# A decoder layer: the product of the context's value and output weights in three rounded products instead of full f32

## Time and profile before

| what | value |
| --- | --- |
| median of the runs shown | 452.72 us |
| the profiled execution's own time | 452.99 us |
| its span in the profile | 451.2 us |
| PE busy | 437.0 us, 97% |
| DVE, ACT, POOL busy | 304.8, 300.9, 210.9 us |

### The profile page before, as it was taken

How to read it: one execution, slowest core, us unless ns; L and a number is a source line. 1 busy time by engine, 2 the same in 40 slices (tenths; PEclk the granted TensorE clock), 3 DMA queues, 4 the chain that set the end, 5 groups by cost and what they waited for, 6 DMA issues and landing times.

```text
span 451.2 us, 11055 instructions
## 1 busy us (share of the span) xinstructions
PE 437.0 (97%) x3657; PEld 394.4 (87%) x3657; DVE 304.8 (68%) x1243; ACT 300.9 (67%) x927; POOL 210.9 (47%) x246
## 2 busy tenths in 40 slices
PE   8999999999999999999999999999999999999991
PEld 7888898989989898898988989899889999999970
DVE  3376666787797575868678677969797734333495
ACT  3688666576777668566686665868665686776535
POOL 1899499250103112210237635375733587666521
PEclk9999999999999999999999999999999999999997
DMA  5960121400210001020001214122023654343675
GB/s 147 323 197 3 64 94 46 142 1 1 95 47 1 1 2 36 24 62 23 1 25 59 83 48 118 48 66 76 26 72 96 165 176 141 121 128 118 215 268 196
DMA packets 26543, 40.16 MB, mean 89 GB/s; under 512 B 3199, under 2 KB 17683, under 8 KB 26483
## 3 DMA queue, kind: packets, MB, share of 16 engines
q1 hardware_dynamic: 21532, 27.86, 20.2%
q0 software_dynamic: 3408, 9.33, 5.8%
q10 hardware_dynamic: 1547, 2.27, 1.7%
HBM read 26.83 MB, written 12.61 MB: 87 GB/s over the span
## 4 chain that ended last, share of the span: by engine, by line
PE 86%; DVE 6%; DMA 3%; ACT 1%; issue 1%; POOL 1%; SPq 1%; ACTq 0%; POOLq 0%
PE bank L310 18%; PE bank L311 18%; PE bank L312 18%; PE bank L829 8%; PE bank L879 7%; PE bank L840 7%; DMA ex_raw<-y_dram 2%; PE bank L1033 2%; PE bank L1057 2%; PE bank L780 2%; PE bank L935 1%; PE bank L757 1%; PE bank L1043 1%; PE bank L1065 1%; DVE stats L1581 1%
## 5 line engine op out<-in xcount | busy, mean ns | idle before, releaser
L1219 ACT ACTIVATE probs<-probs,negmax 128x128 f32<-128x128 f32 x256 | 99.7, 393 | 24.6 <-DVE negmax L1493 24.6
L1493 DVE CUSTOM_DVE_ANT_0 probs<-bank,mask 128x128 f32<-128x128 f32 x256 | 62.4, 285 | 45.5 <-PE bank L829 45.5
L310 PE MATMUL bank<-w_hi,ot_hi 128*128 (+1 forms) x284 | 80.6, 284 | 0.1
L311 PE MATMUL bank<-w_lo,ot_hi 128*128 (+1 forms) x284 | 80.3, 283 | 0.0
L312 PE MATMUL bank<-w_hi,ot_lo 128*128 (+1 forms) x284 | 80.1, 282 | 0.0
L1504 DVE TENSOR_TENSOR probs<-probs,rsum 128x512 f32<-128x512 f32 x64 | 58.7, 917 | 2.2
L310 PE MATMUL bank<-xt_hi,w_hi 128*128 128x512 f32 (+1 forms) x148 | 59.7, 403 | 0.0
L611 POOL DMA_INDIRECT xg_dram<-xacc,place x32 | 33.6, 1051 | 54.4 <-PE bank L840 29.6
L311 PE MATMUL bank<-xt_lo,w_hi 128*128 128x512 f32 (+1 forms) x148 | 57.6, 389 | 0.0
L312 PE MATMUL bank<-xt_hi,w_lo 128*128 128x512 f32 (+1 forms) x148 | 57.5, 389 | 0.0
L310 PEld LDWEIGHTS bank<-w_hi,ot_hi 128*128 128x128 f32 x284 | 54.0, 190 | 0.5 <-issue 0.5
(11 more groups left out here) (252 smaller groups left out, 1056.4 us busy)
## 6 DMA issues: line engine op xcount, KB each, us to landing
qkv<-xg_dram SPq DMA_DIRECT2D x39, 128.5 KB, 2.2
ex_raw<-in_w_experts SPq DMA_DIRECT2D x18, 256.0 KB
w_raw<-in_w_quads SPq DMA_DIRECT2D x10, 256.0 KB, 4.7
xacc<-in_x SPq DMA_DIRECT2D x4, 512.0 KB, 4.1
ex_raw<-in_w_cross SPq DMA_DIRECT2D x4, 512.0 KB, 3.9
w_raw<-in_ctx_t_in ACTq DMA_DIRECT2D x4, 512.0 KB, 3.8
w_raw<-in_w_quads SPq DMA_DIRECT2D x3, 512.0 KB, 6.1
xacc<-in_x_t SPq DMA_DIRECT2D x3, 512.0 KB, 6.9
```

The lines of the kernel that those rows point to most:

```text
L310: pe.matmul(o, a_hi, b_hi, start=first, stop=False)
L311: pe.matmul(o, a_hi, b_lo, start=False, stop=False)
L1219: nc.scalar.activation(tile, tile, ACT.Exp, scale=-1.0, bias=negmax[:, s.par, h, j:j + 1], accum_out=sums[:, s.par, h, j:j + 1]).then_inc( ...
L1493: nc.vector.tensor_tensor_reduce(probs[:, s.par, h, slices(j, P)], sc_bank[h][:, slices(j, P)], mask[:, :], -SCALE, 3.0e38, ALU.add, ALU.m ...
```

## The change

The three products hi hi, hi lo and lo hi of `three` take the place of one full f32 product, four times in each of four steps. POOL splits each block of ex_raw into w_hi and w_lo, in the place of the shared expert (block `NE` = 8, which no quad uses, and which split_expert(0) and (1) fill later). PE waits for the split (cross_split) instead of the load, load_cross waits for the split instead of the product, and POOL's split waits for PE's step before, since it overwrites w_hi. The steps move from behind slots 3 to 6 to behind slots 5 to 8, take_wvo from behind slot 7 to behind slot 8, and wvo_low from inside slot 8 to inside slot 9. The ten row casts of split_rows become join_rows, with split_cross(1) ahead of them.

```diff
@@ load_cross
                 if b > 0:
-                    sp.wait_ge(wvo_step, b)
+                    sp.wait_ge(cross_split, b)
                 sp.dma_start(ex_raw[:, :, :], w_cross[b]).then_inc(in_cross, 16)
@@ gpsimd
+            def split_cross(r):
+                pool.wait_ge(in_cross, 16 * (r + 1))
+                if r > 0:
+                    pool.wait_ge(wvo_step, r)
+                split(w_hi[:, NE, :, :], w_lo[:, NE, :, :], ex_raw[:, :, :], cross_split)
+
@@ split_rows
                     pool.wait_ge(pool_step, 6 + 2 * k)
+            def join_rows():
+                pool.wait_ge(cross_split, 2)
+                raw = rows_raw.rearrange("p (e n) -> p e n", n=D)
                 for r in (32, 96):
                     for k in range((NX + 1) // 2):
@@ gpsimd, the order
             split_part(3, 2)
+            split_cross(0)
             nc.gpsimd.memset(rows_raw, 0.0).then_inc(rows_zeroed, 1)
             tables()
             split_rows()
+            split_cross(1)
+            join_rows()
             add_ob(1)
+            split_cross(2)
             add_ob(2)
+            split_cross(3)
             split_ctx(0)
@@ cross_weights
-                pe.wait_ge(in_cross, 16 * (r + 1))
+                pe.wait_ge(cross_split, r + 1)
                 for i in range(2):
                     for m in range(KT):
-                        mm = pe.matmul(bank[7][:, slices(m, D)], ex_raw[:, 0, i * D + m * P:i * D + (m + 1) * P],
-                                       ex_raw[:, 1, slices(i, D)], start=(r == 0 and i == 0 and m == 0),
-                                       stop=(r == G - 1 and i == 1), skip_group_check=True)
+                        here = slice(i * D + m * P, i * D + (m + 1) * P)
+                        v_hi, v_lo = w_hi[:, NE, 0, here], w_lo[:, NE, 0, here]
+                        o_hi, o_lo = w_hi[:, NE, 1, slices(i, D)], w_lo[:, NE, 1, slices(i, D)]
+                        begin, end = r == 0 and i == 0 and m == 0, r == G - 1 and i == 1
+                        for n, (v, o) in enumerate(((v_hi, o_hi), (v_hi, o_lo), (v_lo, o_hi))):
+                            mm = pe.matmul(bank[7][:, slices(m, D)], v, o, start=(begin and n == 0),
+                                           stop=(end and n == 2), skip_group_check=True)
                 mm.then_inc(wvo_step, 1)
@@ tensor
-            behind = {3 + r: [lambda r=r: cross_weights(r)] for r in range(G)}
+            behind = {5 + r: [lambda r=r: cross_weights(r)] for r in range(G)}
@@ scalar
-            behind = {1: [make_sel], 7: [take_wvo, lambda: load_ctx(0)]}
+            behind = {1: [make_sel], 7: [lambda: load_ctx(0)], 8: [take_wvo]}
@@ vector
-            inside, small = {SPG: [wvo_low]}, {}
+            inside, small = {SPG + 1: [wvo_low]}, {}
```

More of the change, by code:

```diff
@@ L245, in decoder_program @@
         in_xt0 = [sem(f"in_xt0_k{k}") for k in range(KT)]
-        in_quad = [sem(f"in_quad_{n}") for n in "qkvo"]
+        in_quad = [sem(f"in_quad_{n}") for n in "qkv"]
         q_split, k_split, v_split = sem("q_split"), sem("k_split"), sem("v_split")
@@ L272, in decoder_program @@
         bias_moved = sem("bias_moved")
+        cross_split = sem("cross_split")
         rows_zeroed, in_up_rows, in_rows, rows_ready = (sem("rows_zeroed"), sem("in_up_rows"), sem("in_rows"),
```

## The result

Over 20 runs each, the changed kernel took 454.01 us in the median (452.92 to 456.29), the kernel before 453.07 (451.92 to 454.55). The ratio is 1.0026, with a 95% interval of 1.0014 to 1.0039: slower by 1.2 us by the ratio (0.9 by the medians), where 1.0 was forecast. How it comes about is as forecast in the main: PE's steps are shorter, and PE waits for POOL's splits at the third or the fourth of them. How the stalls divide between those two differs from one execution to the next, and one cost was not foreseen at all.

A forecast was written before the change was run, and what follows sets the result against it. PE, busy 97% of the span, was taken to bound the kernel until 322 us. Stalls of 2.3 us less a gain of 1.28 put 1.0 on 452.72, giving 453.7 us, range 451.3 to 455.7.

The forecast's parts named there:

- PE's own gain: PE's four cross_weights steps: 1.82 us becomes 1.50 each, a gain of 0.32 a step, 1.28 us in four.
- When PE asks: Behind slots 5 to 8: PE, without stalls, asks for the four splits at 63.6, 73.7, 84.0 and 94.1 us.
- POOL's chain: GpSimd's queue of splits, row casts and sums: splits ready at 45.45, 73.4, 85.6 and 96.4 us.
- the third pair: split_cross(2) on POOL, a cast and a subtraction: 3.7 us with the gap, ready at 85.6.
- the upper bound: POOL's late case: pairs at 4.0, rows at 52.6, 1 us of collisions; fourth split about 98.9, +3.5 us.
- The stalls: PE waits for POOL's splits: 1.6 us at the third step, another 0.7 at the fourth, 2.3 in all.
- the margin at the second split: split_cross(1) ready at 73.4 against PE's asking at 73.7: no stall, 0.3 us of margin.
- the upper end of POOL's chain: Fourth split at about 98.9 us with pairs, rows and collisions at their slow ends: +3.5 us.
- rival 2: Slot 9: DVE becomes 1.5 us late at add_cross(0,0), PE waits 0.9 more, 454.6 us; chance 0.1.
- PE's cover: DVE's products beside POOL's subtractions may last up to 2.4 + 0.7 us; costed at nothing while PE has no wait.
- Costed at nothing: take_wvo, wvo_low in DVE's slot 9, load_ctx(0), split_ctx(0) and load_expert(0): later, but covered, so no cost.
- a gain of half a microsecond for the rows: SP's queue: load_cross(1) goes at 45.5, so the row loads go from 47.8, 0.5 us earlier.

The follow-up runs named there:

- the version without stalls: Changed kernel, GpSimd takes split_cross(2) between the halves of the row casts and split_cross(3) ahead of add_ob(2): 451.39 us, ratio 0.9963; again 451.45 us, 0.9967.
- that with the third step's alone: Changed kernel with split_cross(3) ahead of add_ob(2) on GpSimd: 453.50 us, ratio 1.0012.

## Why the prediction was right

- *PE's own gain*, 0.32 a step: 0.29 measured in the trace (1.53 for 1.82), and by the runs 1.6 us in four steps, against 1.28.
- *When PE asks*: 63.6, 73.7, 84.0 forecast, 63.8, 73.9, 84.2 measured. The 0.2 is where PE stood at slot 3's end.
- *POOL's chain*: right in its order and links, and light by 1.2 us at the third split. Two terms were mis-sized: the ten row casts, 7.0 for 6.3, and the third pair, 1.53 + 2.88 = 4.5 with the gap for 3.7, both beside DVE's products. They are partly made up for by a second split 0.4 us earlier than forecast. I took the means and gave the collisions to the upper bound alone.
- *The stalls*: "PE stalls 1.6 us" at the third step was 2.7 in one execution and 0.3 in the other; "another 0.7 us" at the fourth was 0 in the one and 0.68 in the other. They trade against each other: all in all 2.7 us in the one, and in the other 1.3, the 50.94 us from slot 4 to slot 9 less the 49.61 of the version without stalls. By the ratios, the version without any stall is at 0.9963 and 0.9967, that with the third step's alone at 1.0012, the changed kernel at 1.0026 and 1.0029: about 2.1 us for the third with what follows it, and 0.7 for the fourth (by itself no more than the noise), 2.8 in all against 2.3, less a gain of 1.6 against 1.28. So that the sum came out within 0.2 us is partly luck: both of its terms were light, and what they lack cancels in part.
- *What I didn't see*: the clock behind a stall, 1.6 us where it fell. That the 2.8 holds some of it is likely, and its share isn't measured. I also took PE's place against POOL's as fixed. Between the two profiles of the changed kernel PE's moves by 0.9 us one way and POOL's second split by 0.9 the other (73.0 and 72.2), where the margin at the second split was 0.3. In PE's timeline 0.2 us of it are there at 28.6 us and 0.4 come with a wait for ScalarE at 35.4 us; the rest was not traced. And the upper end of POOL's chain adds up to 99.1, not 98.9, which changes neither the range nor a chance.
- *DVE* (rival 2): in these slots its longest product went from 2.17 to 2.90 us, beside split_cross(1)'s subtraction, which POOL began at 70.60, and in no profile of the changed kernel did PE wait for it in slots 9 to 11. That is the lock of the Trainium skill, "SBUF — State Buffer", section "SBUF: two separate sides": the trace agrees, with 2.90 us where 2.4 + 0.7 was the most by it. PE's cover held. The version with all splits in time has the same four splits and lost nothing to it.
- *Costed at nothing*: no wait of PE came from the moved steps, wvo_low or the context's and experts' loads. But I read the new wait of load_cross as a gain of half a microsecond for the rows, where the move without it cost 6.3 us.

## What to carry to other kernels

When work for the bounding engine is made cheaper by preparing its operands on another engine, write down for each piece when it is asked for and when the other engine's whole queue, with the loads that stand in it, lets it be ready; the order in that queue was worth 2.7 us here, more than the cheaper product. Look at the next step too when a stall is taken away at one: here POOL's load, sum and split took 12.1 us between two steps 10.3 us apart, and 1.5 of the 2.7 us came back. Before a step is moved later, look at what each in-order DMA queue holds behind the wait that the step releases.

## What the hardware showed that I had not expected

- After PE idled for 2.5 us or more in the midst of its work (2.50, 2.50, 2.85, 4.94 in four profiles), its granted clock went to 0.5 for some 3 us, at a cost of 1.6 us where it was added up; after 0.68 to 1.50 it stayed at 1.00.
- POOL's casts of single rows of 512 elements, 0.61 us in the median, also lengthen, up to 1.07, beside DVE's operations on two SBUF tiles: ten took 6.23 us before, with one such operation among them, and 7.02 after, with two. DVE's product of 0.69 took up to 2.90 beside a subtraction of 2.42 on POOL.
